# A new order of work on all five engines of a four-block graph network, with one transpose moved ahead of a weight load in the opening

## What is computed

```python
h = relu(layernorm(x)); x = x + attention(h, adj, Wq, Wk, Wv)              # 12 heads, masked by adj: "first"
h = relu(layernorm(x)); x = x + directed(h, adj, W_left, W_self, W_right)  # "single"
h = relu(layernorm(x)); x = x + directed(directed(h, ...), ...)            # two layers: "lower", then "upper"
h = relu(layernorm(x)); x = x + attention(h, adj as bias, Wq, Wk, Wv) @ Wo.T + bo   # "last"

def directed(h, adj, ...):
    a = softmax(h @ h.T / sqrt(384)) * adj
    a = a / (a.sum(-1) + 1e-10)
    c = upper(a) @ left(h) + diag(a) * own(h) + lower(a) @ right(h)
    return relu(layernorm(c) * gain + offset)
```

## Time and profile before

| | us |
|---|---|
| median of 3 runs | 2410.92 |
| lowest and highest run | 2410.62, 2415.63 |
| the profiled execution | 2413.84 |
| its span, first to last instruction | 2412.1 |

### The profile page before, as it was taken

How to read it: one execution, slowest core, us unless ns; L and a number is a source line. 1 busy time by engine, 2 the same in 40 slices (tenths; PEclk the granted TensorE clock), 3 DMA queues, 4 the chain that set the end, 5 groups by cost and what they waited for, 6 DMA issues and landing times.

```text
span 2412.1 us, 78687 instructions
## 1 busy us (share of the span) xinstructions
PE 2277.4 (94%) x25872; PEld 1658.4 (69%) x25872; DVE 1912.4 (79%) x8824; ACT 1844.8 (76%) x4660; POOL 1752.6 (73%) x2322
## 2 busy tenths in 40 slices
PE   2689999999999999999999999999999999999984
PEld 2457777777777777777777777777777777777753
DVE  6768878888888888888888888888888888888863
ACT  4458887878888887878888787888878788877853
POOL 2147777777778777877777787777777777777763
PEclk7799999999999999999999999999999999999996
DMA  8213434443444444343444434443434444353322
GB/s 208 54 30 68 81 69 85 75 83 67 82 80 72 80 77 81 69 86 72 76 76 81 79 71 83 76 80 69 84 76 74 78 76 82 69 85 73 73 49 53
DMA packets 597158, 185.87 MB, mean 77 GB/s; under 512 B 563728, under 2 KB 596752, under 8 KB 596752
## 3 DMA queue, kind: packets, MB, share of 16 engines
q1 hardware_dynamic: 596752, 180.84, 40.2%
HBM read 29.76 MB, written 12.58 MB: 18 GB/s over the span
## 4 chain that ended last, share of the span: by engine, by line
PE 77%; DVE 7%; DMA 6%; issue 3%; SPq 3%; POOL 2%; ACT 1%; DVEq 0%; ACTq 0%; POOLq 0%
PE bank L147 19%; PE bank L148 19%; PE bank L149 19%; PE bank L1488 4%; PE bank L1542 3%; DMA pT<-p 3%; PE bank L1529 3%; DMA raw_weights_of_out<-raw_weights 3%; SPq L499 2%; PE bank L1504 1%; PE bank L1506 1%; PE bank L1505 1%; PE bank L1587 1%; PE bank L1584 1%; PE bank L1585 1%
## 5 line engine op out<-in xcount | busy, mean ns | idle before, releaser
L147 PE MATMUL bank<-w_hi,dir_hT_hi 128*128 128x384 f16 x1728 | 564.5, 327 | 0.0
L148 PE MATMUL bank<-w_lo,dir_hT_hi 128*128 128x384 f16 x1728 | 564.5, 327 | 0.0
L149 PE MATMUL bank<-w_hi,dir_hT_lo 128*128 128x384 f16 x1728 | 564.3, 327 | 0.0
L796 ACT ACTIVATE probs<-minus_scores,minus_max 128x128 f32<-128x128 f32 x1536 | 484.5, 390 | 64.7 <-DVE minus_max L1043 64.6
L660 POOL TENSOR_TENSOR p<-probs,p 128x512 f16<-128x512 f32 x384 | 445.8, 1161 | 51.3 <-ACT p L803 51.1
L147 PE MATMUL bank<-hT,w_hi 128*128 128x128 f16 x2304 | 400.3, 220 | 18.6 <-DMA hT<-h 15.7
L148 PE MATMUL bank<-hT,w_hi 128*128 128x128 f16 x2304 | 400.3, 220 | 0.0
L149 PE MATMUL bank<-hT,w_lo 128*128 128x128 f16 x2304 | 400.2, 220 | 0.0
L1043 DVE CUSTOM_DVE_ANT_0 minus_scores<-bank,minus_score_bias 128x128 f32<-128x128 f32 x1536 | 343.1, 285 | 17.2 <-issue 8.9
L149 PEld LDWEIGHTS bank<-w_hi,dir_hT_lo 128*128 128x128 f16 x1728 | 169.4, 98 | 112.4 <-issue 1.0
L148 PEld LDWEIGHTS bank<-w_lo,dir_hT_hi 128*128 128x128 f16 x1728 | 169.4, 98 | 112.4 <-issue 1.0
(11 more groups left out here) (174 smaller groups left out, 7135.5 us busy)
## 6 DMA issues: line engine op xcount, KB each, us to landing
x<-in_x SPq DMA_DIRECT2D x64, 192.0 KB, 2.7
out<-raw_weights SPq DMA_DIRECT2D x64, 192.0 KB, 2.2
pT<-p SPq DMA_TRANSPOSE x384, 3.2
adj_tile<-in_adj SPq DMA_DIRECT2D x64, 64.0 KB, 2.3
hT<-h SPq DMA_TRANSPOSE x128, 2.7
raw_weights<-in_L_gnn_Wq SPq DMA_DIRECT2D x2, 576.0 KB, 5.0
raw_weights<-in_L_gnn_Wk SPq DMA_DIRECT2D x2, 576.0 KB, 6.2
raw_weights<-in_L_gnn_Wv SPq DMA_DIRECT2D x2, 576.0 KB, 7.2
```

The source lines that it names most:

```text
L147: pe.matmul(out, stat[0], move[0], start=first, stop=False)
L148: pe.matmul(out, stat[0], move[1], start=False, stop=False)
L149: return pe.matmul(out, stat[1], move[0], start=False, stop=last)
L796: last = act.activation(probs[:, i, :], scores[:, i, :], ACT.Exp, bias=nmax[:, t.slot(), i:i + 1], scale=-1.0)
```

## The change

The list of tasks of every engine is put in another order, in the round and in the opening. No arithmetic, tile or transfer is added or removed. One wait is added: `scaled_eps` waits for the previous task's `cvar_ready`, since it may now run before `context` of its own layer. Many calls `wait(engine, ...)` become `engine.wait_ge(...)` with the same semaphore and value. In the round, the first part of `n_.last(3)` moves to the end of the round before (`probs_lo`, `turn_probs` of chunk 0, the exponentials of chunk 1), as do the tail of the upper layer and `turn_e` and `project_right` of the lower layer; `project_v` of "last" moves the other way. The core of the diff:

```diff
 # SP, the round
-                    turn_probs(n_.last(3), 2)
-                    turn_probs(n_.last(3), 0)
-                    turn_probs(n_.last(3), 1)
                     load_x(n_.first(-2))
                     att_load_adj(n_.first(-2))
+                    turn_probs(n_.last(3), 1)
+                    turn_probs(n_.last(3), 2)
                     turn_h(n_.last(2))
+                    write(n_.last(4))
                     turn_o(n_.last(3))
...
-                    write(n_.last(4))
                     turn_h(n_.first(-2))
+                    turn_probs(n_.last(2), 0)
 # SP, the opening
                 turn_probs(first[0], 2)
+                turn_h(first[1])
                 W1.ready(sp)
                 W2_upper.load_matrices(sp)
                 W2_upper.load_vectors(sp)
-                turn_h(first[1])
                 load_x(first[2])
 # POOL, the opening
-                add_v_bias(first[0])
+                att_norm(first[1])
                 probs_lo(first[0], 0)
                 probs_lo(first[0], 1)
                 probs_lo(first[0], 2)
-                att_norm(first[1])
                 att_lo(first[1])
+                add_v_bias(first[0])
                 add_attended(first[0])
 # POOL, the round, its end
+                    add_v_bias(n_.first(-1))
                     fold_scores(n_.last(2))
+                    probs_lo(n_.last(2), 0)
+                    context_norm(n_.upper(1))
                     add_attended(n_.first(-1))
+                    gain(n_.upper(1))
 # ACT, the round, its end
                     dir_turned_hi(n_.lower(0))
-                    att_normed(n_.first(-2))
-                    att_hi(n_.first(-2))
                     exponents(n_.last(2), 0)
+                    probs_hi(n_.last(2), 0)
                     exponents(n_.last(2), 2)
                     exponent(n_.lower(0))
                     left_hi(n_.lower(0))
-                    probs_hi(n_.last(2), 2)
-                    probs_hi(n_.last(2), 0)
+                    norm_context(n_.upper(1))
+                    exponents(n_.last(2), 1)
 # DVE, the opening
                 score_bias(first[0])
+                att_stats(first[1])
+                att_mean_var(first[1])
                 biased_max(first[0], 0)
...
                 W2.find_max(dve)
-                att_stats(first[1])
-                att_mean_var(first[1])
+                att_var_eps(first[1])
                 v_lo_split(first[0])
                 W1.bias_rows_low(dve, ROW["single"])
                 W1.split_low(dve)
-                att_var_eps(first[1])
 # DVE, the round, its end
                     biased_max(n_.last(2), 0)
-                    dir_turned_lo(n_.lower(0))
                     biased_max(n_.last(2), 1)
                     biased_max(n_.last(2), 2)
+                    dir_turned_lo(n_.lower(0))
                     context(n_.upper(1))
                     row_sums(n_.first(-1))
+                    context_stats(n_.upper(1))
                     row_max(n_.lower(0))
+                    context_mean_var(n_.upper(1))
                     row_scales(n_.first(-1))
-                    scaled_eps(n_.upper(1))
                     minus_row_max(n_.lower(0))
+                    context_var_eps(n_.upper(1))
                     attended_rows(n_.first(-1))
                     mask(n_.lower(0))
                     left_lo(n_.lower(0))
 # PE, the round: the new list as it stands after the change
+                    project_v(n_.last(3)); project_k(n_.first(-1)); dir_turn_h(n_.single(0)); combine(n_.lower(1))
+                    project_q(n_.first(-1)); project_left(n_.single(0)); similarity(n_.single(0)); score(n_.first(-1))
+                    attend(n_.last(3), 0); attend(n_.last(3), 1); project_right(n_.single(0)); turn_e(n_.single(0))
+                    attend(n_.last(3), 2); project_self(n_.single(0)); dir_turn_h(n_.upper(1)); project_v(n_.first(-1))
+                    combine(n_.single(0)); similarity(n_.upper(1)); project_left(n_.upper(1)); project_q(n_.last(2))
+                    project_k(n_.last(2)); turn_e(n_.upper(1)); project_right(n_.upper(1)); project_out(n_.last(3))
+                    score(n_.last(2)); project_self(n_.upper(1)); attend(n_.first(-1), 0); dir_turn_h(n_.lower(0))
+                    attend(n_.first(-1), 1); combine(n_.upper(1)); attend(n_.first(-1), 2); similarity(n_.lower(0))
+                    project_left(n_.lower(0)); project_self(n_.lower(0)); turn_e(n_.lower(0)); project_right(n_.lower(0))
 # scaled_eps
+                    wait(dve, d["cvar_ready"], t.count(-1))
```

More of the change, by code:

```diff
@@ L686, in step @@
                 def step(n_):
+                    offset(n_.upper(2))
+                    dir_norm(n_.single(0))
+                    sides_lo(n_.lower(1))
+                    probs_lo(n_.last(3), 1)
                     probs_lo(n_.last(3), 2)
                     fold_again(n_.last(3))
-                    dir_norm(n_.single(0))
-                    sides_lo(n_.lower(1))
-                    context_norm(n_.upper(2))
-                    probs_lo(n_.last(3), 0)
-                    gain(n_.upper(2))
-                    probs_lo(n_.last(3), 1)
-                    offset(n_.upper(2))
+                    att_norm(n_.last(2))
                     context_norm(n_.lower(1))
@@ L1265, in step @@
-                    scaled_denominator(n_.lower(1))
-                    diagonal(n_.lower(1))
-                    context_var_eps(n_.upper(2))
-                    right_lo(n_.lower(1))
-                    score_sums(n_.last(3))
-                    context(n_.lower(1))
-                    dir_turned_lo(n_.single(0))
-                    scaled_eps(n_.lower(1))
-                    context_stats(n_.lower(1))
-                    v_lo_split(n_.last(3))
-                    context_mean_var(n_.lower(1))
+                    right_lo(n_.lower(1))
@@ new lines, in step @@
+                    add_to_x(n_.upper(2))
+                    score_bias(n_.first(-1))
+                    scaled_denominator(n_.lower(1))
+                    att_stats(n_.last(2))
+                    v_lo_split(n_.last(3))
+                    dir_turned_lo(n_.single(0))
+                    context(n_.lower(1))
+                    scaled_eps(n_.lower(1))
+                    att_mean_var(n_.last(2))
+                    context_stats(n_.lower(1))
+                    att_var_eps(n_.last(2))
@@ L1276, in step @@
+                    context_mean_var(n_.lower(1))
+                    context_var_eps(n_.lower(1))
+                    score_sums(n_.last(3))
+                    att_stats(n_.first(-2))
                     row_max(n_.single(0))
-                    context_var_eps(n_.lower(1))
+                    left_lo(n_.single(0))
+                    nonzero_sums(n_.last(3))
                     minus_row_max(n_.single(0))
+                    score_bias(n_.last(2))
+                    att_mean_var(n_.first(-2))
@@ L1279, in step @@
+                    biased_max(n_.first(-1), 0)
                     mask(n_.single(0))
-                    add_to_x(n_.upper(2))
-                    left_lo(n_.single(0))
-                    biased_max(n_.first(-1), 0)
                     biased_max(n_.first(-1), 1)
                     part_sides(n_.single(0))
+                    diagonal(n_.single(0))
                     biased_max(n_.first(-1), 2)
-                    diagonal(n_.single(0))
-                    att_stats(n_.last(2))
+                    att_var_eps(n_.first(-2))
@@ L1409, in _ @@
                 W2_upper.split_low(dve)
-                att_stats(first[2])
-                att_mean_var(first[2])
+                v_lo_split(first[1])
+                drop_masked(first[2])
                 add_to_x(single[0])
@@ L1624, in step @@
                     project_left(n_.lower(0))
-                    project_v(n_.last(2))
                     project_self(n_.lower(0))
+                    turn_e(n_.lower(0))
+                    project_right(n_.lower(0))
                 def turn_v_bias(pe):
@@ L1683, in _ @@
                 W3.ready(pe)
+                attend(first[1], 0)
                 dir_turn_h(lower[0])
-                attend(first[1], 0)
                 attend(first[1], 1)
@@ L1690, in _ @@
                 project_self(lower[0])
+                turn_e(lower[0])
+                project_right(lower[0])
                 run_rounds(step)
```

339 lines of the change are left out of this document (164 added, 175 removed).

## The result

The changed kernel takes 2381.8 us (median of four runs, 2380.0 to 2382.5), the kernel before beside it 2413.3 (2410.6 to 2417.5). The ratio is 0.987, with a 95% interval of 0.985 to 0.989: 31.5 us less, 1.3%. The forecast was 2398, some 12 us less, with a range of its own from 2390 to 2406 and a wide one from 2386 to 2425. The sign was right, the size was not. The profiled execution took 2382.45 us, with a span of 2380.5 (before: 2413.84 and 2412.1).

What follows compares the result with a forecast made beforehand. PE was taken to bound full rounds, a chain through all engines the last 72 us. Opening -8.6 + 0.2, PE's time 0, DMA waits -2, drain -2 gave -12.4: 2398 us, own range 2390 to 2406, wide 2386 to 2425.

Steps and rivals of the forecast that it cites:

- What bounds it: Full rounds: PE is the bound; a better order can give back some 12 to 15 us and no more.
- The full rounds, DMA waits: Full rounds: most `pT` waits go, `turn_o` waits grow +5 to +6; net -2 us, bounds -8 and +6.
- The opening: Before the first full round: `project_k` of graph 1 starts 8.6 us earlier; -8.6, bounds -3 and -11; DVE cost 0.2.
- The rival that all of it would be swallowed: After the opening: the DVE chain, `find_max` above all, swallows its gain, rounds give 4; 2407, chance 0.08.
- PE's own time: Full rounds: same matmuls in another sequence, joins differ slightly; 0 us, bounds -6 and +6.
- The end of the round: From X, the start of `similarity(lower)`, to `project_right`: `left_lo` ready at X+3.3 to 3.6, PE doesn't wait; 0 us.
- the POOL rival: End of the round: `row_scales` held by POOL's `probs_lo`, PE waits 0.2 us a round; +12, 2410, chance 0.17.
- The slower rival: Full rounds: hand-over before `similarity(lower)` or `combine(upper)` 0.5 us late each round, PE loses 31 us; 2429, chance 0.18.
- The added wait: On `scaled_eps`: the `cvar_ready` it waits for was set several tasks before; 0, bound 0.1 us a round.
- The drain: Last graph: `context_norm` freed from `fold_again`, about 1.0 of 2.2 us, turns about 1; sum -2, bounds 0 and -4.
- The other term, 1.0 for the last three turns: Drain: chunk 0's exponentials, high and low part in a row; turns start 1.2 us earlier, end about 1 earlier.
- The rival "the waits nearly vanish": Full rounds: turned rows don't come later, their waits nearly vanish, opening gives a few us more; 2389, chance 0.07.

Runs made afterwards that it cites:

- turn_o_later: Changed kernel with `attended_hi(last)` behind `v_hi_split(first)` on ACT, so `turn_o` is issued later: 2395.3 us, 0.992 of the kernel before.
- turn_o_sooner: Kernel before with `attended_lo(last)` ahead of `att_stats(first)` on DVE, so `turn_o` is issued sooner: 2399.4 us, ratio 0.994.
- turn_moved: Kernel before with one line moved: SP issues `turn_h` of graph 1 ahead of `W1.ready` and the W2_upper loads: 2406.2 us, ratio 0.9974.
- turn_back: Changed kernel with `turn_h` of graph 1 moved back behind the W2_upper loads on SP: 2389.7 us, 0.990 of the kernel before.
- max_first: Changed kernel with `biased_max` 1 and 2 of graph 1 ahead of `W2_upper.find_max` on DVE: 2384.2 us, 0.988 of the kernel before.
- scales_first: Changed kernel with `row_scales` of the first attention ahead of `row_max` on DVE at the round's end: 2406.1 us, 0.9975 of the kernel before.

## Why the prediction was wrong, and where it was right

**What bounds it** was right: PE in full rounds, DMA waits as all that there is to gain in them. It said "some 12 to 15 us and no more", and 15.0 came. It then forecast 2 of these. By the distances of starts from 300 to 2280 us the waits before `attend(first, 2)` and `project_out` were 10.2 and 7.0 us and are now 0 and 4.2: 13.0 of the 15.0. The view of waits, from which the forecast was made, shows only 12.1 of these 17.2 us.

**The step that failed** is "The full rounds, DMA waits", and in it the second half. Right was that `turn_o` would be issued later against its reader: 3.63 us in the median, forecast 3.4 to 3.5, before 3.97. Right was that the `pT` waits would go. Wrong was the sentence "So the ten to twelve rounds that waited wait 0.5 longer each". It took the landing times as given, a property of the DMA, and changed only the room. But the landings are late where a packet stands at a certain distance from the issue, and the new order changed that distance. In the kernel before, packets stood at +1.75 to +2.2 us of `turn_o` in 11 of 55 rounds, just where they do most harm; in the changed kernel they stand at +0.4 to +1.3 in 11 and at +2.2 to +2.7 in 10, where most of them do little. Five rounds wait for 3.3 us instead of ten for 4.4. The term was +5 to +6 and measured -1 in the view of waits, -3 by the distances of starts. The same step can be redone with the measured room: the landings of the kernel before exceed 3.98 us by 5.9 us in all and would exceed 3.63 by 10.1, which is the forecast's kind of loss; the landings that came exceed it by 3.9. That the packets fell where they did is luck, nobody had planned it: turn_o_later, with 0.4 us less room, loses 13.6 us.

For `pT` the reason was also only half right. The prediction gave it to `dir_turn_h` and `combine` between chunks 1 and 2. By the new list only `combine` is between these two, `dir_turn_h` is between chunks 0 and 1, and both stood ahead of all three attends before. What `attend(first, 2)` gained, from 4.2 to 5.4 us behind its issue, comes, by the lists, with `project_self(upper)`, now ahead of the attends; no run took that apart. The room alone is enough for the waits to go: no landing of chunk 2 in the kernel before took over 5.3 us. And turn_o_sooner gets rid of the same waits without any change on PE.

**The opening**: forecast 8.4, measured 6.3 (turn_moved) and 7.9 (turn_back) for the line, 6.8 for all its lists alone; 11.7 in the two traces, of which some 3 are chance that goes with the granted clock of that stretch. The turn of graph 1 was issued at 48.95 (forecast 49.8), `project_k` started at 52.1 (forecast 52.6). What was said to be late next was the W2 split and then the `find_max`; it was so, as max_first showed, and took 2 of the 9 us. The rival that all of it would be swallowed is out.

**PE's own time**: forecast 0 with bounds of 6. The shortest rounds, in which no turn is late, take 34.67 us after and 34.68 before: 0.01 to 0.02 * 58, about 1 us less. Within the bounds; it was not tested by a run.

**The end of the round**: the forecast took POOL to be out of the way, with `left_lo` at X + 3.3 to 3.6; with POOL in the way it gave X + 3.95. Found are X + 3.85, and PE at X + 3.9, due at 3.86. So the POOL rival, with a chance of 0.17, is what happened: `row_scales` takes 0.91 us instead of the 0.25 expected without it. It was over-priced, since it costs 0.05 us a round instead of 0.2. So the forecast's 0 came nearly right (0.05 * 58 = 3 us) for a reason that it had not: `left_lo` is 0.1 us sooner than in the rival. PE has no more than that to spare, as scales_first shows. The slower rival, a late `dir_turned_lo`, had 0.2 us of room by the forecast and has 0.22 in the trace (27.45 against 27.67 us into the round); it didn't happen.

**The added wait**: 0 forecast. DVE has 191 more waiting instructions, and from 300 to 2200 us PE waits for none of them.

**The drain**: forecast 2, bounds 0 and 4, measured 4.9. The step that was too small is `context_norm` behind `fold_again`. I took 1.0 of 2.2 us, since `att_norm(last)` would stand behind `fold_again` instead. It was 3.9, in two parts. Before, DVE reached `context` of the last graph only behind all of `biased_max`, 2.77 us after `combine(upper)` began on PE at 2359.10, and POOL came to `context_norm` (2366.39) 2.6 us after its variance was ready. DVE before:

```profile
2361.87 0.55 DVE L1224 TENSOR_TENSOR raw_weights<-bank,raw_weights 128x384 f32<-128x384 f32 x1
...
2363.64 0.14 DVE L1245 TENSOR_SCALAR cvar_eps<-cmean_var 128x1 f32<-128x1 f32 x1
```

In the changed kernel `context` comes 1.27 us after `combine`, and `context_norm` 0.1 us after the variance. DVE, then POOL:

```profile
2335.27 0.14 DVE L1246 TENSOR_SCALAR cvar_eps<-cmean_var 128x1 f32<-128x1 f32 x1
```

```profile
2334.37 1.15 POOL L660 TENSOR_TENSOR p<-probs,p 128x512 f16<-128x512 f32 x1
2335.49 0.55 POOL L645 TENSOR_TENSOR cln_scale_bias<-cvar_eps,minus_half 128x1 f32<-128x1 f32 x1
...
2341.69 0.99 POOL L628 TENSOR_TENSOR raw_weights<-raw_weights 128x384 f32<-128x384 f32 x1
2342.64 0.55 POOL L584 TENSOR_TENSOR ln_scale_bias<-var_eps,minus_half 128x1 f32<-128x1 f32 x1
```

`att_norm` loses only 0.4 us behind `fold_again`, and from `combine(upper)` to `project_q(last)` of graph 63 it is 16.65 us instead of 20.5. In four traces with the new rounds it is 16.64 to 16.66, in four with the old 20.47 to 20.51, so this is no chance; no run took the two parts apart. The other term, 1.0 for the last three turns, came as forecast: 25.5 us from `project_q(last)` to `project_out` instead of 26.4.

**The range**: three terms came out better together, 3 us in the opening, 13 in the rounds and 3 in the drain. In the two traces all three lie beyond their bounds, 11.7 against 11, 13.0 against 8 and 4.9 against 4, so the bounds themselves were too near. The rival "the waits nearly vanish", 2389 with a chance of 0.07, came nearest. Its effect was right, its condition was not: the turned rows do come later against their reader, and the waits shrink all the same.

## What to carry to other kernels

A wait for a DMA that appears in one round of four need not be noise: set its issue against the packets of the instruction queues first. A step of half a microsecond for the issue can then weigh as much as a new order on five engines: 14 us gained in one place here, 14 lost in another, against the 15 of the new order's full rounds. It is tried by one swap of neighbours. To foresee its size is another matter: the five forecasts made here from the packets' places missed by 3 to 10 us. An earlier issue is the safer side, for it gives room wherever the packets stand. Where slack is forecast for a landing, use the late landing time and not the median, and ask what makes it late.

## What the runs showed of the hardware

- A transposing DMA of 192 KB that takes 2.74 us lands 1.0 us later in the median when one 16-KB packet of PE's instruction stream starts 0.9 us behind its issue, and 1.7 us later at 2.1 us (`turn_o`). Behind 2.3 us one in five is late. In the view shown the turns all but stand still for 1.1 us, with no more than a tenth of the 16 DMA engines' time in use. Without an instruction packet near it none of 1125 turns was over 0.05 us late.
- The Trainium skill (Trainium Architecture — The Big Picture, The software stack) says that the instruction streams are brought into the engines when a program is loaded. The trace shows that this is not the whole of it, with 208 packets of PE's stream through the execution.
- PE's stream of 53,000 instructions comes in 208 packets of 16 KB, 13 for four rounds. The late landings of `turn_o` in the kernel before are mostly four rounds, 140 us, apart (500, 640, 779 us).
- Two semaphore waits share one instruction: 12 waits added 6 instructions, 48 added 24.
- A DVE task of 12 columns (128x12, float32) takes 0.20 us with POOL at rest and 1.20 beside a POOL task of 1.16 us that begins with it; begun 0.28 us later it takes 0.91. In each case it ends with POOL's.
